# Edge list of a graph network padded from 53125 to 53248 edges, cut into 416 columns of 128 instead of 425 columns of 125

## What is computed

```python
edge_index = jnp.stack([src, dst])
h = jnp.maximum(_layernorm(x, axis=-1), 0.0)
x = x + _L0_gnn_ref(h, edge_index, edge_attr_64, ...)  # MLP of 512 on each edge, summed by dst, MLP on the nodes, layer norm
h = jnp.maximum(_layernorm(x, axis=-1), 0.0)
x = x + _L1_gnn_ref(h, edge_index, edge_type_64, ...)  # attention, 4 heads, softmax over the edges of a dst
h = jnp.maximum(_layernorm(x, axis=-1), 0.0)
x = x + _L2_gnn_ref(h, edge_attr_64, ..., edge_index)  # attention, 8 heads, softmax over all edges; dst and src trade places
h = jnp.maximum(_layernorm(x, axis=-1), 0.0)
x = x + _L3_gnn_ref(h, edge_index, ...)                # attention, 1 head, then an LSTM gate on the nodes
```

## Time and profile before

| what | value |
|---|---|
| median of three runs | 5657.19 us |
| runs | 5649.09, 5657.19, 5662.35 us |
| span of the profiled execution, first to last instruction | 4326.7 us |
| median less span | 1330.5 us |
| busy: PE, DVE, POOL, ACT | 66%, 68%, 68%, 21% of the span |
| mean granted TensorE clock | 0.836 of full speed |
| HBM traffic | 533 MB read, 59 MB written |

### The profile page before, as it was taken

One profiled execution on the slowest core, in us unless ns is written; L12 is line 12 of the kernel. 1 busy time (PEld: TensorE's weight loads), 2 busy tenths in 40 slices (PEclk: granted clock), 3 DMA queues, 4 the chain that ended last, 5 costly groups with the idle time before them and its releaser, 6 DMA issues. The chain is left out here.

```text
span 4326.7 us, 58090 instructions
## 1 busy us (share of the span) xinstructions
PE 2839.9 (66%) x13396; PEld 1634.1 (38%) x13396; DVE 2936.0 (68%) x6725; ACT 910.5 (21%) x2606; POOL 2939.7 (68%) x2929
## 2 busy tenths in 40 slices
PE   5144588888887998588888976688888852000007
PEld 4144332222222886345445543355555532000004
DVE  7497448888886333477778866477777776666664
ACT  0011111111111332234344421122222212000004
POOL 0477667777775777677777747677777736777772
PEclk8555699999998999799999988799999976555558
DMA  3244336666667333566666723466666633444441
GB/s 163 31 122 139 86 113 187 187 189 188 187 189 162 56 61 61 139 174 173 179 175 181 202 62 69 124 194 190 190 187 192 190 85 94 108 108 107 108 105 39
DMA packets 408483, 594.57 MB, mean 137 GB/s; under 512 B 266671, under 2 KB 272980, under 8 KB 407356
## 3 DMA queue, kind: packets, MB, share of 16 engines
q0 software_dynamic: 185552, 519.27, 43.6%
q1 hardware_dynamic: 222828, 74.02, 7.4%
HBM read 532.97 MB, written 59.28 MB: 137 GB/s over the span
## 5 line engine op out<-in xcount | busy, mean ns | idle before, releaser
L1721 PE MATMUL edge_psS<-edge_terms,ident 128*128 128x256 f32 x1936 | 497.1, 402 | 124.9 <-DVE edge_psS L1764 124.5
L1109 POOL DMA_INDIRECT edge_ring<-tab,edge_rec x480 | 462.6, 964 | 146.3 <-issue 143.9
L2060 POOL DMA_INDIRECT state<-tab,edge_rec x480 | 455.2, 948 | 155.1 <-issue 146.0
L1721 PEld LDWEIGHTS edge_psS<-edge_terms,ident 128*128 128x128 f32 x1936 | 371.5, 198 | 336.4 <-DVE edge_psS L1764 263.0
L1631 POOL DMA_INDIRECT state<-tab,edge_rec x360 | 342.9, 953 | 154.5 <-issue 103.0
L2233 PE MATMUL gate_psA<-ident,gate_w_nat 128*128 128x128 f32 x8 | 2.0, 428 | 633.1 <-DMA gate_w_nat<-in_L_gnn_W_ih 633.1
L1631 POOL DMA_INDIRECT state<-tab,edge_feat x360 | 341.5, 949 | 109.8 <-issue 107.0
L1740 PE MATMUL edge_psX<-state,ident 128*128 128x512 f32 x720 | 352.9, 613 | 69.2 <-DMA state<-tab,edge_feat 66.6
L1171 DVE TENSOR_TENSOR edge_ring<-edge_psX,edge_ring 128x1024 f32<-128x1024 f32 x240 | 293.9, 1225 | 135.4 <-PE edge_psX L1152 91.2
L1795 DVE TENSOR_TENSOR edge_prod<-edge_psX,state 128x1024 f32<-128x1024 f32 x240 | 293.4, 1223 | 135.6 <-PE edge_psX L1740 135.4
L1143 PE MATMUL edge_psX<-state,ident 128*128 x720 | 370.5, 624 | 0.0
(11 more groups left out here) (449 smaller groups left out, 6325.6 us busy)
## 6 DMA issues: line engine op xcount, KB each, us to landing
sorted_d<-state SPq DMA_DIRECT2D x7, 2380.0 KB
state<-src_rows SPq DMA_DIRECT2D x25, 562.5 KB
state<-low_rows SPq DMA_DIRECT2D x25, 562.5 KB
state<-tab,edge_rec POOLq DMA_INDIRECT x840, 2.8
edge_ring<-tab,edge_rec POOLq DMA_INDIRECT x600, 3.6
update_row_out<-in_edge_attr SPq DMA_DIRECT2D x40, 156.2 KB
edge_rec<-rec_d SPq DMA_DIRECT2D x364, 8.0 KB, 2.9
state<-tab,edge_feat POOLq DMA_INDIRECT x360, 3.7
```

The lines of the kernel that those rows point to most:

```text
L1109: pool.indirect_dma_start(out=ring[:, k, s, :], out_offset=None, in_=S["tab0"][:, :], in_offset=bass.IndirectOffsetOnAxis(ap=rec[:, k, R_S ...
L1721: last = pe.matmul(so_far, S["ident"][:, :], terms[:, s, :], start=False, stop=(s == QE - 1), skip_group_check=True)
L2060: pool.indirect_dma_start(out=ring[:, k, s, :], out_offset=None, in_=S["tab3"][:, :], in_offset=bass.IndirectOffsetOnAxis(ap=rec[:, k, R_S ...
```

## The change

The list is padded with 123 edges to 53248 = 416 x 128. The padding edges carry node number 3327, whose high part 25 matches no node block; their rows go to 128 extra rows at the end of `sorted_d`. `EDGE_P` is now 128, `EDGE_C` 416, `COLS` 16 (26 turns instead of 25), and the one-hot tiles have no unused column. The first loads use 104 rows of 4 x 128 numbers. A group of the row scatter has `HERE` = 4 columns: 12 groups in `make_tables`, 55 in `update_nodes`, 12 in `attend` and 25 in `project_out`. The rings keep their lengths. Scatters by stage were 50, 200, 60, 115 and are 48, 220, 48, 100. In `attend` the scatters now stand behind steps 1 to 4. Memsets of the unused column and partitions go, one blank DMA of 128 rows and one small addition come.

```diff
-EDGE_P = 125
-EDGE_C = N_EDGES // EDGE_P
-SPAN = 85
-COLS = 17
-HERE = 5
-WIDE = COLS + 1
+EDGE_P = P
+EDGE_C = -(-N_EDGES // EDGE_P)
+N_PAD = EDGE_C * EDGE_P
+SPAN = 104
+COLS = 16
+HERE = 4
+NO_NODE = NB * P + P - 1
...
-UPDATE_GROUPS, PROJECT_GROUPS = 40, 23
-ROW_TURNS = 12
+MAKE_GROUPS, UPDATE_GROUPS, ROW_TURNS = 12, 55, 12
+PROJECT_GROUPS = EDGE_C // HERE - MAKE_GROUPS - UPDATE_GROUPS - ROW_TURNS
...
-                pool.iota(S["number"][:, :, :], [[1, P], [0, WIDE]], base=0, channel_multiplier=0, **kw).then_inc(s_iota, 1)
+                pool.iota(S["number"][:, :, :], [[1, P], [0, COLS]], base=0, channel_multiplier=0, **kw).then_inc(s_iota, 1)
...
+                sp.dma_start(S["sorted_d"][SORTED_ROWS:SORTED_ROWS + P, :], blank[:, 0:SROW]).then_inc(s_pd, 16)
...
-                for to in (dlo, dhi):
-                    step(dve.memset(to[:, :, :], 0))
...
-                for to in (src_h, slo, shi):
-                    step(dve.memset(to[:, :, :], 0))
...
-                    dve.tensor_tensor(oh_lo[0:EDGE_P, h, :, :], number[0:EDGE_P, :, :], bc(slo[:, t, :], 1, [EDGE_P, P, WIDE]), ALU.is_equal).then_inc(s_oh, 1)
+                    dve.tensor_tensor(oh_lo[0:EDGE_P, h, :, :], number[0:EDGE_P, :, :], bc(slo[:, t, :], 1, [EDGE_P, P, COLS]), ALU.is_equal).then_inc(s_oh, 1)
...
+                step(dve.tensor_tensor(place[:, EDGE_C - 1:EDGE_C], place[:, EDGE_C - 1:EDGE_C], dump[:, :], ALU.add))
...
-    dram("src_rows", [EDGE_C // COLS, EDGE_P, WIDE], I16)
-    dram("low_rows", [EDGE_C // COLS, EDGE_P, WIDE], BF16)
+    dram("src_rows", [EDGE_C // COLS, EDGE_P, COLS], I16)
+    dram("low_rows", [EDGE_C // COLS, EDGE_P, COLS], BF16)
...
-    dram("sorted_d", [SORTED_ROWS, SROW])
+    dram("sorted_d", [SORTED_ROWS + P, SROW])
...
-        ROWS_AT, ROWS_N = 0, 0 if gat else 10
+        ROWS_AT, ROWS_N = 0, 0 if gat else MAKE_GROUPS
...
-    longer = lambda v: np.concatenate([v, np.zeros((QE - 1,) + v.shape[1:], v.dtype)])
+    longer = lambda v, of: np.concatenate([v, np.full((N_PAD - N_EDGES,) + v.shape[1:], of, v.dtype)])
```

More of the change, by code:

```diff
@@ L324, in _ @@
                         dve.wait_ge(s_used, t - 1)
-                    step(dve.tensor_tensor(oh_hi[:, h, :, :], S["number"][0:EDGE_P, 0:NB, :], bc(dhi[:, t, :], 1, [EDGE_P, NB, WIDE]), ALU.is_equal))
-                    dve.tensor_tensor(oh_lo[:, h, :, :], S["number"][0:EDGE_P, :, :], bc(dlo[:, t, :], 1, [EDGE_P, P, WIDE]), ALU.is_equal).then_inc(s_oh, 1)
+                    step(dve.tensor_tensor(oh_hi[:, h, :, :], S["number"][0:EDGE_P, 0:NB, :], bc(dhi[:, t, :], 1, [EDGE_P, NB, COLS]), ALU.is_equal))
+                    dve.tensor_tensor(oh_lo[:, h, :, :], S["number"][0:EDGE_P, :, :], bc(dlo[:, t, :], 1, [EDGE_P, P, COLS]), ALU.is_equal).then_inc(s_oh, 1)
                 dve.wait_ge(s_used, TURNS)
@@ L417, in rank_edges @@
     FIRST = 9
-    EVEN = EDGE_C + 1
+    EVEN = EDGE_C + 2
     MAKE_AT = 6
@@ L436, in rank_edges @@
         place = ph.sb("place", [EDGE_P, EDGE_C])
+        dump = ph.sb("dump", [EDGE_P, 1])
         deg = ph.sb("deg", [P, NB])
@@ L505, in _ @@
                         sp.dma_start(row[:, h, 0:EDGE_P, :].rearrange("p n c -> p (n c)"),
-                                     rows_of(S["src_rows"][t, :, :].rearrange("p c -> (p c)"), EDGE_P * WIDE)).then_inc(s_row[h], 16)
+                                     rows_of(S["src_rows"][t, :, :].rearrange("p c -> (p c)"), EDGE_P * COLS)).then_inc(s_row[h], 16)
                     else:
                         sp.dma_start(row_b[:, h, 0:EDGE_P, :].rearrange("p n c -> p (n c)"),
-                                     rows_of(S["low_rows"][t, :, :].rearrange("p c -> (p c)"), EDGE_P * WIDE)).then_inc(s_row[h], 16)
+                                     rows_of(S["low_rows"][t, :, :].rearrange("p c -> (p c)"), EDGE_P * COLS)).then_inc(s_row[h], 16)
                     if u == TURNS + MAKE_AT + 2:
@@ L646, in _ @@
                 step(dve.tensor_scalar(part_i, S["src_i"][:, :], 7, None, ALU.logical_shift_right))
-                step(dve.tensor_copy(shi[:, :, 0:COLS], folded(part_i)))
+                step(dve.tensor_copy(shi[:, :, :], folded(part_i)))
                 step(dve.memset(one_b[:, :], 1.0))
                 step(dve.memset(zeros[:, :], 0.0))
-                step(dve.memset(row[:, :, EDGE_P:P, :], 0))
                 step(dve.memset(rec[:, :, :], 0))
                 step(dve.memset(scan[:, :, 0:1], 0.0))
+                step(dve.tensor_scalar(dump[:, :], S["iota_p"][:, 0:1], float(N_EDGES - (EDGE_C - 1) * EDGE_P), float(SORTED_ROWS), ALU.is_ge, ALU.mult))
                 step(dve.tensor_scalar(later[:, :, :], number[0:EDGE_P, :, :], S["iota_p"][0:EDGE_P, 0:1], None, ALU.is_gt))
-                step(dve.memset(later[:, EDGE_P:P, :], 0.0))
                 for t in range(TURNS):
@@ L851, in shared_by_lists @@
     sb("tri", [P, P])
-    sb("number", [P, P, WIDE], BF16)
+    sb("number", [P, P, COLS], BF16)
     sb("x_row", [P, NB], I32)
@@ L1551, in attend @@
         AHEAD, TURNED = 4, 2
-        scattered = RowScatter(ph, S, A, 10 + UPDATE_GROUPS, ROW_TURNS, 1) if layer == 1 else None
+        scattered = RowScatter(ph, S, A, MAKE_GROUPS + UPDATE_GROUPS, ROW_TURNS, 1) if layer == 1 else None
         away = ph.sb("away", [P, 4, QE, ED if layer == 1 else 1])
```

53 lines of the change are left out of this document (27 added, 26 removed).

## The result

The kernel after took 5721.27 us in the median of four runs (5716.02 to 5745.55), the kernel before 5653.14 (5644.13 to 5662.35): a ratio of 1.0151, 95% interval 1.0103 to 1.0200. The change made the kernel 1.5% slower. The forecast was 5502 us, a gain of 155.

The account below looks back on a forecast made before the run. The prediction took the number and length of POOL's DMAs to set update_nodes and project_out; terms -4 - 10 - 8 - 24 - 62 - 47 = -155 us took 5657 to 5502 us, range 5475 to 5562.

Parts of the forecast that it names:

- I take the 1330 us around it as unchanged: Whole run: 1330 us of the median lie outside the profiled span of 4326.7 us and stay.
- C: Rival, update_nodes: SP's destination loads as slow as at a stage's start, +163 us there, total +32, 5689 us; chance 0.03.
- Scatter of 128 rows: Row scatters on POOL: 0.96 us instead of 1.18, so 1.26 with issue instead of 1.48.
- B: Rival, row scatters: 128 rows scatter no faster than 125, total -60 us, 5597 us; chance 0.07.
- A: Rival, update_nodes: the ring of two groups starves POOL, +21 us instead of -24, total -110, 5547 us; chance 0.14.
- make_tables: Stage make_tables: 23 scatters instead of 25 ahead of the first table store in POOL's queue, -8 us.
- attend 1: Attend, layer 1: the wait for the record load goes, turns of 45.1 us instead of 50.07, -62 us.
- update_nodes: Stage update_nodes: POOL's chain 308 us against 331, POOL staying last by little, -24 us.
- project_out: Stage project_out: POOL's chain of scatters and stores 157 us against 204.2, -47 us.
- rank_edges: Stage rank_edges: quicker put, shorter one-hots, DVE's gain mostly turned into waiting for gathers, -10 us, bounds -3 and -20.
- the upper case: Stage rank_edges: POOL's gathers follow DVE's shorter loop, so the stage gains nearer 12 us; otherwise 3.
- First steps and order_nodes: Counting stages: one-hots of 2048 elements instead of 2304, shorter iota and casts, fewer memsets, -4 us.

Follow-up runs that it names:

- c_before: The kernel before, unchanged, as a control on chip 4 in the fast group: 4316.47 us.
- c_after: The kernel after, unchanged, as a control on chip 4 in the fast group: 4179.05 us, ratio 0.9679 to the kernel before.
- c_before2: The kernel before, unchanged, once more, on chip 3 in the slow group: 5512.98 us.
- e_step5: The kernel after with attend 1's scatters behind steps 2 to 5 instead of 1 to 4, slow group: 5627.48 us, ratio 1.0178 to the kernel before.
- e_scat125: The kernel after with row scatters moving 125 of the 128 rows of a column, slow group: 5480.51 us, ratio 0.9925 to the kernel before.
- g_early: The kernel before with attend 1's five scatters behind steps 0 to 4 instead of 1 to 5, fast group: 4284.70 us, ratio 0.9928 to the kernel before.
- g_noscat: The kernel after with the loads and scatters of update_nodes' 55 groups left out, fast group: 4177.99 us.
- d_noscat: The kernel after with the loads and scatters of update_nodes' 55 groups left out, slow group: 5558.75 us.

## Why the prediction was wrong

**The step that failed is the first one**, "I take the 1330 us around it as unchanged". They did not lie around the span. The timed runs were executions in which the same instructions take 1330 us longer inside it. So every later term was read from stages whose bound is another one in the runs that count. How the stages stand, in us, from the barriers between them in four traces (c_before, c_after, c_before2, after):

| stage | before, fast | after, fast | before, slow | after, slow | forecast |
|---|---|---|---|---|---|
| first steps, order | 175.1 | 167.5 | 176.0 | 167.2 | -4 |
| rank_edges | 290.5 | 278.4 | 466.1 | 473.2 | -10 |
| make_tables | 135.1 | 129.7 | 136.2 | 140.8 | -8 |
| edge_mlp | 783.7 | 780.7 | 1026.0 | 1055.3 | 0 |
| update_nodes | 355.9 | 339.5 | 406.0 | 533.4 | -24 |
| attend 1 | 764.9 | 708.8 | 989.6 | 1032.7 | -62 |
| project_out | 226.0 | 194.8 | 227.7 | 223.3 | -47 |
| attend 2 | 778.6 | 777.7 | 1101.1 | 1136.0 | 0 |
| the rest | 802.2 | 800.3 | 968.6 | 981.9 | 0 |
| span | 4312.0 | 4177.4 | 5497.2 | 5743.8 | -155 |

The two slow traces are of different batches, in which before differs by 2% or so, and a term under 30 us can't be read from them. On one chip, e_step5 less c_before2 gives +101 in `update_nodes`, +38 in `attend` 1, -3 in `project_out`, -7 and +6 in the counting stages, and +13 in `edge_mlp`, which the change does not touch. Two things happened. POOL's queue does not set the end of the three large stages in the slow group (with longer scatters, e_scat125 has them 122, 13 and 21 us shorter than e_step5), so the 104 us that the three large terms gained in the fast group came to nothing. And the shape of scatter that is faster on POOL is the one with which PE's ends come later there: with 125 rows in the same kernel the loss is gone (5480.51 us for 5532.22 of before). Neither of the two was among the rivals; C, the slower one, had the loads of a group at fault, which were quick (SP's queue of a group 1.7 us in after).

**Point by point in the fast group**, where the sum of -155 measured -134.6 on the span (4312.0 to 4177.4):

*Scatter of 128 rows*, 0.96 us: right, and B wrong. *The ring of two* (A): POOL waited for a group's load 1.87 us once early in `update_nodes` and 0.52 and 0.89 us in its middle; A did not come; SP's queue for a group took 1.7 to 1.8 us, between the two rates of the forecast. *make_tables*: -5.4 for -8.

*attend 1*: the rows of POOL for the first scatter of two turns:

```profile
1714.42 0.98 POOL L780 DMA_INDIRECT sorted_d<-edge_row_out,edge_row_idx  x1 [0.30 <-issue]
...
1759.66 0.98 POOL L780 DMA_INDIRECT sorted_d<-edge_row_out,edge_row_idx  x1 [0.30 <-issue]
```

A turn of 45.2 us, forecast 45.1, for the 50.07 of the earlier trace rows, with no wait for a record load in it: -56 for -62. g_early shows that 30 of these come from the place alone.

*update_nodes*: -16.4 for -24. The term took POOL's chain as the end ("so POOL stays last, by little"), and by little it did. Its last store in c_after, and DVE's wait for one of the three buffers that POOL's stores set free:

```profile
1686.41 1.08 POOL L1246 DMA_INDIRECT tab<-update_next_row,lane_i  x1 [0.30 <-DVE update_next_row L1297]
...
DVE update_next_row L1297 <- DMA tab<-update_next_row,lane_i: 2.6, 1, 2.6
```

From the first scatter (1373.65) to this store are 313 us for the forecast's 308, 2.5 of the rest in the waits for loads; and from the store's end to the barrier 8.9 us pass, where c_before has 5.5. But 24 could not be had in any case: g_noscat shows the other engines' floor at 337, 2.4 us under what was measured and 19 under before. I had seen PE's 321 busy us and did not ask what its rounds need without POOL.

*project_out*: -31.2 for -47, since here the others did come last. The end of POOL's queue:

```profile
2573.36 1.23 POOL L1246 DMA_INDIRECT tab<-project_next_row,lane_i  x1 [0.30 <-issue]
2581.03 0.96 POOL L1246 DMA_INDIRECT tab<-project_next_row,lane_i  x1 [6.44 <-DVE project_next_row L1297]
2590.03 0.95 POOL L1246 DMA_INDIRECT tab<-project_next_row,lane_i  x1 [8.04 <-DVE project_next_row L1297]
2593.57 0.96 POOL L1246 DMA_INDIRECT tab<-project_next_row,lane_i  x1 [2.59 <-DVE project_next_row L1297]
```

17 us of waiting for DVE's rows, where the earlier trace rows had 0.30 of issue: without them the term would be right.

*rank_edges*: -12.1 for -10, inside its bounds.

```profile
182.34 1.22 DVE L661 TENSOR_TENSOR state<-state,rank_src_h 128x2048 bf16<-128x2048 int16 x1 [2.50 <-DMA state<-src_rows]
...
363.41 0.43 DVE L629 CAST state<-state 128x512 f32<-128x512 int32 x1 [12.78 <-DMA state<-in_edge_sr,rank_edge_i]
```

The put of `src_rows` and `low_rows` took 7.2 us for 18.6, the first wait fell from 13.79 to 2.50 us, and DVE's lead went into the wait for POOL's gathers, 12.78 for 6.44. The forecast of some 15 was near. The 128 gathers took 187.2 us in c_after for 200.2 in c_before: they set the stage, and the 12 us of the upper case, in which they follow DVE's shorter loop, is what came. *First steps and order_nodes*: -7.6 for -4, 3.4 of it ahead of `order_nodes`.

The Trainium skill, DMA: Bandwidth & Descriptors, section on why a DMA increments its semaphore by 16, has the rule by which 128, 64, 121, 125 and 127 partitions use 16, 16, 11, 5 and 1 engines. The runs agree with it for scatters, on the packets above and on POOL's time (1.185 us for 125 rows, 2.542 for 127, 0.964 for 128).

**What stays open** is what a late end is. Two facts bound it. The trace of after has 28,228 semaphore updates where c_after, the same program, has 71,851; it has about as many as c_after only in the stages that take as long (813 and 819 in `order_nodes`, 756 and 758 in `gate_nodes`, and 1457 and 1455 in `update_nodes` of d_noscat and g_noscat, from barrier to barrier). And in stretches of the slow traces an engine starts one instruction each 0.7 us or a multiple. PE in the first loop of `rank_edges` of after, a loop of 342 us in place of 158 up to its end:

```profile
237.77 0.20 PE L557 MATMUL rank_psH<-rank_oh_hi,rank_oh_lo 128*128 128x25 bf16 x1 [2.60 <-issue]
240.57 0.20 PE L557 MATMUL rank_psH<-rank_oh_hi,rank_oh_lo 128*128 128x25 bf16 x1 [2.60 <-issue]
243.37 0.20 PE L557 MATMUL rank_psH<-rank_oh_hi,rank_oh_lo 128*128 128x25 bf16 x1 [2.60 <-issue]
```

The Trainium skill, NOTIFIC — the notification-queue block, section 7.1, says that the block which takes the trace's records holds back inside itself rather than lose a record there, and that this could throttle an engine. That would fit the even pace, though not by itself the missing records, and would make the slow group a matter of recording. Since every execution here has a recorded span and clock, none can show it, and I don't claim it.

## What to carry to other kernels

When the span of a profile and the time of the runs differ as much as here (4327 and 5657 us; in every later run 1.7 to 2.2 us), suspect that the profile is of another kind of execution: say so, and don't add the difference as a constant. Before giving an engine's saving to the stage, ask what the others need for it without that engine; an experiment that leaves the work out (g_noscat) answers it in one run. The number of partitions of an indirect DMA bears on its time on POOL: 64, 128 and 121 cost 0.91 to 1.01 us here, 125 cost 1.19 and 127 cost 2.54. But the quicker shapes were the slower kernel in the slow group, so a gain read from one engine's rows has to be measured where the kernel will run.

## What the runs showed that I had not expected

- POOL's time for a scatter hardly depends on how many rows it has, but fits the rows of the busiest engine: 0.906 us for 64 rows, 0.964 for 128, 1.185 for 125, 2.542 for 127.
- One program takes 4179 us in a batch on chip 4 and 5744 in one on chip 1, with the same busy time of DVE (2926 and 2927 us) and a granted clock of 0.847 and 0.750. Which of two kernels is faster depends on the group: 0.968 in one batch, 1.015 and 1.023 in two others.
- In the slow group `update_nodes` takes 335 us without scatters, 385 with scatters of 125 rows and 499 to 534 with 64, 121 or 128, though these take less of POOL's time than those of 125.
